# First x in four tiles, identity matmuls from the beginning, ctx's half of the gate sums ahead of x's, decode chunks and statistics placed anew

## The reference, cut to what matters

```
q = layernorm(x);  k = v = ctx                      # x, ctx: (8, 256, 512)
z = concat([q, k, v])                               # 1536 wide
ig, fg = z @ Wi + bi, z @ Wf + bf                   # the "gate sums": 2 x 16 columns
F = cumsum(log_sigmoid(fg));  log_D = tril(F_s - F_t) + ig_t
D = exp(log_D - max_t log_D);  C = (q @ k.T / sqrt(32)) * D     # per head
h = C / (max(|sum C|, exp(-max)) + 1e-6) @ v;  h = normed per head * ln_scale
x = x + h
w_gu, w_down = fp4(gate_up_packed) * scales, fp4(down_packed) * scales
g, u = split(layernorm(x) @ w_gu.T);  y = (silu(g) * u) @ w_down.T
out = x + y / rms(y)
```

## Time and profile before

| | |
|---|---|
| three runs | 546.90, 548.03, 548.43 us; median 548.03 |
| the profiled execution | 549.5 us, of it the span of the trace 547.8 us |
| mean granted clock of TensorE | 0.984 |
| PE busy | 507.3 us (93%) |
| DVE busy | 391.2 us (71%) |
| first feed-forward matmul of the span | 108.72 us after its start |

### The profile page before, as it was taken

The page is one execution under the profiler, slowest core; times in us unless marked ns, Lnnn a source line. Parts: engine busy times, 40 slices in busy tenths (PEclk is TensorE's granted clock), DMA queues, the critical chain, the costliest instruction groups (busy, mean ns, idle before and its releaser), DMA issues.

```text
span 547.8 us, 8218 instructions
## 1 busy us (share of the span) xinstructions
PE 507.3 (93%) x2752; PEld 280.2 (51%) x2752; DVE 391.2 (71%) x691; ACT 295.1 (54%) x639; POOL 332.2 (61%) x371
## 2 busy tenths in 40 slices
PE   0989996899999899999999999999999989989996
PEld 0556773436666345466665445566664443323442
DVE  4877878978888988277778898477778763877301
ACT  0355854387776352677767234787764224865000
POOL 1054446188887763667776883667768653888501
PEclk9988997999999999999999999999999999999999
DMA  8854037073103200456006001571000000200000
GB/s 270 245 175 167 9 109 256 33 258 136 40 2 134 97 0 2 130 186 225 0 7 227 0 1 41 193 269 39 2 1 1 19 20 25 90 1 1 20 19 38
DMA packets 22234, 47.81 MB, mean 87 GB/s; under 512 B 1840, under 2 KB 8880, under 8 KB 21680
## 3 DMA queue, kind: packets, MB, share of 16 engines
q1 hardware_dynamic: 22192, 47.28, 25.1%
HBM read 37.31 MB, written 4.33 MB: 76 GB/s over the span
## 4 chain that ended last, share of the span: by engine, by line
PE 73%; DVE 12%; ACT 5%; issue 4%; POOL 4%; DMA 1%; DVEq 0%; POOLq 0%; ACTq 0%
PE pf L993 25%; PE pf L979 18%; PE po L917 9%; PE pq L883 7%; PE pq L842 2%; PE pq L895 2%; PE pq L979 2%; PE pf L1012 2%; PE pq L922 2%; DVE ffn L1258 2%; ACT dmat L664 2%; DVE ffn L1262 1%; POOL hT L540 1%; ACT ts L698 1%; DVE bst L1081 1%
## 5 line engine op out<-in xcount | busy, mean ns | idle before, releaser
L993 PE MATMUL pf<-w_down,hT 128*128 128x512 f32 x352 | 154.0, 595 | 1.7 <-DVE w_down L1326 1.7
L979 PE MATMUL pf<-yT,gu_val 128*128 128x512 f16 x552 | 133.5, 380 | 4.5 <-DVE ffn L1262 1.7
L535 POOL TENSOR_TENSOR ffn<-ffn,ts 128x512 f32<-128x512 f32 x88 | 118.3, 1345 | 28.7 <-DVE ffn L1262 18.7
L698 ACT ACTIVATE ts<-pf,gu_scale 128x512 f32<-128x512 f32 x138 | 87.3, 684 | 46.8 <-PE pf L979 45.6
L993 PEld LDWEIGHTS pf<-w_down,hT 128*128 128x128 f32 x352 | 65.8, 190 | 83.8 <-issue 77.3
L979 PEld LDWEIGHTS pf<-yT,gu_val 128*128 128x128 f16 x552 | 49.9, 98 | 67.8 <-DVE ffn L1262 8.3
L664 ACT ACTIVATE dmat<-negm,aT 128x128 f32<-128x128 f32 x248 | 77.7, 396 | 0.8 <-DMA negm<-negm_dram 0.8
L540 POOL TENSOR_TENSOR hT<-ffn,th 128x512 f32<-128x512 f32 x44 | 57.7, 1314 | 28.9 <-DVE th L1271 28.9
L1258 DVE SCALAR_TENSOR_TENSOR ffn<-pf,gu_scale,ts 128x512 f32<-128x512 f32 x69 | 51.6, 748 | 32.7 <-PE pf L979 18.7
L917 PEld LDWEIGHTS po<-v_sb,dmat 128*128 128x128 f32 x512 | 62.1, 192 | 4.8 <-issue 0.4
L494 POOL TENSOR_SCALAR_AFFINE_SELECT dmat<-dmat 128x512 f32<-128x512 f32 x64 | 44.2, 705 | 27.1 <-ACT dmat L664 27.1
(11 more groups left out here) (124 smaller groups left out, 650.9 us busy)
## 6 DMA issues: line engine op xcount, KB each, us to landing
negm<-negm_dram SPq DMA_DIRECT2D x31, 512.0 KB, 5.2
ffn<-in_x SPq DMA_DIRECT2D x4, 1024.0 KB, 6.7
xT<-in_ctx_T SPq DMA_DIRECT2D x16, 256.0 KB, 6.0
ctx_sb<-in_ctx SPq DMA_DIRECT2D x4, 1024.0 KB, 5.7
x_sb<-in_x SPq DMA_DIRECT2D x4, 1024.0 KB, 5.5
x_res<-x_sb SPq DMA_DIRECT2D x4, 1024.0 KB, 5.4
out<-x_res SPq DMA_DIRECT2D x16, 256.0 KB, 2.2
ts<-in_gate_up_bytes SPq DMA_DIRECT2D x4, 352.0 KB, 9.5
```

The source lines that it names most:

```text
L535: pool.tensor_tensor(acc, acc, ts[:, h % TDEEP, 1], ALU.add).then_inc(tsum_ready, 1)
L698: act.activation(ts[:, h % TDEEP, g], bank(q, h, g), ACT.Copy, scale=gu_scale[:, g * GU + o:g * GU + o + 1]).then_inc(t_ready, 1)
L979: last = pe.matmul(bank(q, h, g), gu_val[:, h // 2 + h % 2 * FT, g], yT[:, part, g], start=(part == 0), stop=(part == 1))
L993: last = pe.matmul(pf[:, tt], hT[:, j, tt * P:(tt + 1) * P], w_down[:, j], start=(j == 0), stop=(j == FT - 1))
```

## The change

1. x of pair 0 is loaded by four transfers of one tile each, every one with its own semaphore (`load_first`), and each tile's statistics wait for its own tile.
2. ctxT comes in another layout (made on the host side of the program, as before) so that each pair is one transfer of 8 KB a partition. This holds for all pairs.
3. PE begins with 28 identity matmuls, does ctx's half of the gate sums, then the transposes of x, then x's half, and then 28 identity matmuls in place of 24.
4. `gate_weights` goes ahead of `norm1` on DVE. Two decode chunks (in place of four) stand before the gate rows, three more between `read_a(0)` and the first unit, and the loop's chunks start with chunk 5 in place of 4, so that they end one unit earlier.
5. The statistics of pair 1's x move from before the first unit to h = 9, 11, 13 and 15 of the loop; `shift1` moves from h = 15 to 17.
6. `head_sums` is split in two; in the first iteration the half of batch entry 0 stands at h = 17.
7. SP loads the scales and does `spread_negm(0)` before the words of the down projection, `ln_row` and pair 1's x.

```diff
-UP_FIRST = 4
-UP_EARLY = 4
+UP_FIRST = 2
+UP_EARLY = 5
 DOWN_CHUNKS = 4
 WORDS_AT = {1 + 2 * i: UP_EARLY + i for i in range(UP_CHUNKS - UP_EARLY + DOWN_CHUNKS)}
+STATS_AT = {9 + 2 * i: i for i in range(TT)}
...
-                for k in range(KT):
-                    sp.dma_start(xT[:, KT + k].rearrange("q (b s) -> q b s", b=2), ctxT_pairs[p][:, k]
-                                 ).then_inc(s_ctxT, 16)
+                sp.dma_start(xT[:, KT:2 * KT].rearrange("q k s -> q (k s)"), ctxT[p]).then_inc(s_ctxT, 16)
+
+            def load_first():
+
+                for tt in range(TT):
+                    sp.dma_start(xg[:, tt], x_pairs[0][:, tt]).then_inc(s_first[tt], 16)
...
-            load_xg(0, None)
+            load_first()
             sp.dma_start(w_gate[:], w_gates).then_inc(s_const, 16)
             sp.dma_start(bias_col[:], b_gates).then_inc(s_const, 16)
             load_gu(0)
             load_ctxT(0)
             load_ctx(0)
             load_gu(1)
-            load_xg(1, None)
             sp.dma_start(sc_raw[:], gu_scales).then_inc(s_scales, 16)
+            spread_negm(0)
             for half in range(2):
                 sp.dma_start(dn_words[half * HALF:(half + 1) * HALF].rearrange("p o w -> p (o w)"), dn_bytes
                              ).then_inc(s_down, 16)
             sp.dma_start(ln_row[:], ln_scale.partition_broadcast(P)).then_inc(s_ln, 16)
-            spread_negm(0)
+            load_xg(1, None)
             iteration(0, None, 1)
...
+            def first_sums(ks):
+
+                if ks[0] == KT:
+                    pe.wait_ge(wg_ready, 1)
+                    pe.wait_ge(s_ctxT, 16)
+                for k in ks:
+                    if k < KT:
+                        pe.wait_ge(xT_read, k + 1)
+                    last = gate_step(k, k == KT, k == KT - 1)
+                if ks[-1] == KT - 1:
+                    last.then_inc(g_done, 1)
...
             pe.wait_ge(const_ready, 2)
+            keep_busy(28, po[:])
+            first_sums(range(KT, 2 * KT))
             turn_x(0)
-            gate_sums(0)
-            keep_busy(24, po[:])
+            first_sums(range(KT))
+            keep_busy(28, po[:])
             spread_first(0)
...
-            def head_sums(p):
-                po_steps.start(p)
-                dve.wait_ge(osq_ready, 2 * p + 2)
-                po_steps.inc(dve.tensor_reduce(hn[:, 0], osq, AX.X, ALU.add))
+            def head_sums(p, b):
+                if b == 0:
+                    po_steps.start(p)
+                dve.wait_ge(osq_ready, 2 * p + 1 + b)
+                g = slice(b * 2 * NH, (b + 1) * 2 * NH)
+                po_steps.inc(dve.tensor_reduce(hn[:, 0, g], osq[:, g], AX.X, ALU.add))
...
-                    if q is None and h == 15:
+                    if q is None and h in STATS_AT:
+                        norm1_sums(n, (STATS_AT[h],))
+                    if q is None and h == 17:
                         shift1(n)
+                        head_sums(p, 0)
                 if q is None:
-                    head_sums(p)
+                    head_sums(p, 1)
                     head_scale(p)
...
             norm1_sums(0)
+            gate_weights()
             norm1(0)
-            gate_weights()
             for i in range(UP_FIRST):
                 decode_up(i)
             gate_rows(0)
...
             read_a(0)
-            norm1_sums(1)
+            for i in range(UP_FIRST, UP_EARLY):
+                decode_up(i)
             iteration(0, None, 1)
```

More of the change, by code:

```diff
@@ L112, in xattn_ffn @@
     ctx_pairs = ctx.rearrange("(p b) (c q) d -> p q (b c) d", b=2, q=P)
-    ctxT_pairs = ctxT.rearrange("(p b) (k q) s -> p q k b s", b=2, q=P)
     out_pairs = out.rearrange("(p b) (c q) d -> p q (b c) d", b=2, q=P)
@@ L232, in xattn_ffn @@
         s_x = sem("s_x")
+        s_first = [sem(f"s_first{i}") for i in range(TT)]
         s_xg = sem("s_xg")
@@ L330, in load_ctxT @@
                     sp.wait_ge(qk_done, UNITS * p)
-                for k in range(KT):
-                    sp.dma_start(xT[:, KT + k].rearrange("q (b s) -> q b s", b=2), ctxT_pairs[p][:, k]
-                                 ).then_inc(s_ctxT, 16)
+                sp.dma_start(xT[:, KT:2 * KT].rearrange("q k s -> q (k s)"), ctxT[p]).then_inc(s_ctxT, 16)
+            def load_first():
+                for tt in range(TT):
+                    sp.dma_start(xg[:, tt], x_pairs[0][:, tt]).then_inc(s_first[tt], 16)
             def load_xg(p, q):
-                if p > 0:
-                    sp.wait_ge(xT_done, KT * p)
+                sp.wait_ge(xT_done, KT * p)
                 sp.dma_start(xg, x_pairs[p]).then_inc(s_xg, 16)
@@ L831, in gate_sums, with gate_step @@
                 pe.wait_ge(xT_read, KT * (p + 1))
[L832 to L835, removed]
+                pe.wait_ge(s_ctxT, 16 * (p + 1))
+                if p > 1:
                     pe.wait_ge(acc_ready, 4 * FT * (p - 1))
                 for k in range(2 * KT):
[L839 to L843, removed]
-                last.then_inc(g_done, 1)
+                    last = gate_step(k, k == 0, k == 2 * KT - 1)
+                last.then_inc(g_done, 1)
+            def first_sums(ks):
[8 more added lines that the diff above has]
+                    last.then_inc(g_done, 1)
+            def gate_step(k, first, final):
+                for gate in range(2):
+                    for b in range(2):
+                        r = (2 * gate + b) * DH
+                        last = pe.matmul(pm[r:r + DH, 0:S], w_gate[:, k, gate * DH:(gate + 1) * DH],
+                                         xT[:, k, b * S:(b + 1) * S], start=first, stop=final)
+                return last
             def turn_back(p):
@@ L1087, in norm1_sums @@
                     g1.start(p)
-                    dve.wait_ge(s_xg, 16 * p + 16)
+                    if p > 0:
+                        dve.wait_ge(s_xg, 16 * p)
                 for tt in tiles:
+                    if p == 0:
+                        dve.wait_ge(s_first[tt], 16)
                     stats(g1, xg[:, tt], 0, tt)
@@ L1433 @@
     scales = _np.asarray(inputs["L0_ffn_gate_up_scales"]).reshape(KT, GU, HALF, 2)
+    ctx_T = _np.asarray(inputs["ctx_2048"]).reshape(PAIRS, 2, S, KT, P).transpose(0, 4, 3, 1, 2).reshape(PAIRS, P, KT * 2 * S)
     inputs = dict(
-        inputs, ctx_T=_np.asarray(inputs["ctx_2048"]).transpose(0, 2, 1), gate_weights=gates, gate_biases=biases,
+        inputs, ctx_T=ctx_T, gate_weights=gates, gate_biases=biases,
         gate_up_bytes=_np.ascontiguousarray(up.transpose(3, 0, 2, 1)).reshape(HALF, GU * KT * P).view(_np.int32),
```

## The result

The changed kernel is slower: median 554.05 us of four runs (553.49 to 554.62) against 548.23 (546.90 to 548.55), ratio 1.0111 with a 95% interval of 1.0089 to 1.0132. Ten runs of it over two sessions lie between 552.2 and 560.9.

A forecast was written before the change was run, and what follows sets the result against it. PE, busy 93% of the span, bounds the later iterations, so only the stretch before the first feed-forward matmul can move. Terms 2.0 - 0.3 - 0.7 - 1.4 + 3.1 = 2.7 us gained, median 548.03 to 545.3; range 541.6 to 547.8.

The forecast's parts named there:

- The start: Up to the end of pair 0's gate sums (G): G at 22.0 us, gain 2.0 (bounds 1.1 and 4.8).
- The 28 matmuls behind G: Identity matmuls after pair 0's gate sums: nearly hidden, 0.3 us lost (0 to 1.3).
- the high-clock rival: Clock stays high from the front matmuls: gate sums end at 19.2, time 542.2 us; chance 0.25.
- Three decodes before unit 0: DVE's decode chunks between the scans and unit 0: 0.7 us late (0 to 1.2).
- Statistics in the units: Pair 1's statistics in slots h = 9, 11, 13: 1.4 us lost (0.6 to 1.6), including a PE wait of 0.6.
- The last unit and head sums: From unit 7's products to the end of head sums: gain 3.1 us (2.3 to 3.3).
- The 1.15 for half of head sums: Half of head sums moves into DVE's wait for PE in the last unit: 1.15 of 2.29 us gained.
- SP's order: Order of SP's loads, with scales early: worth nothing.
- The slower one: Rival: the 28 identity matmuls behind the gate sums run slow and outlast the scans, 551.6 us; chance 0.08.

The follow-up runs named there:

- g2: e3 with the scales loaded ahead of pair 1's x, as in the changed kernel; 546.72 us, ratio 0.9970 to the kernel before.
- e2: The changed kernel with PE's list at the start as before the change (transposes, then all gate sums); 550.38 us, ratio 1.0037.
- g3: The changed kernel without the 28 identity matmuls in front, ctx's half still first; 553.52 us, ratio 1.0104.
- g4: g2 with PE's order of e2, three decode chunks ahead of the gate rows, one behind the scans, half of head sums at h = 17; 544.28 us, ratio 0.9938.
- f3: The changed kernel with 14 identity matmuls in place of 6 between unit 0's scores and its values; 550.76 us, ratio 1.0066.
- h1: g2 with pair 1's statistics at h = 9, 11, 13 and 15 and shift1 at h = 17; 552.78 us, ratio 1.0070.
- e3: The changed kernel with decodes, statistics and SP's order put back, head sums in two pieces behind the last step; 551.19 us, ratio 1.0066.
- the second profile: The changed kernel itself run and profiled once more, nothing changed; median 552.64 us, ratio 1.0089.
- e4: The kernel before with five decode chunks ahead of the gate rows, statistics in the units and head sums in halves; 551.78 us, ratio 1.0055.
- f2: The changed kernel with three decode chunks ahead of the gate rows and two behind the scans; 551.76 us, ratio 1.0008.

## Why the prediction was wrong

I forecast 545.3, in a range up to 547.8, and the time is 554.05. Point by point:

- *The start.* Right: G 22.2 where I had 22.0, nm 6.6 later, ctxT at 14.3 inside the bounds, ctx's half slow and x's half fast. g2 confirms the size (1.6). The 28 matmuls behind G lost nothing (0.3 forecast). The G of the high-clock rival (19.2) is real too, G at 18.5, but it comes from transposes in front and not from identity matmuls (e2, g3, g4).
- *Three decodes before unit 0: "I take 0.7 late (0 to 1.2)".* **This is the first step that failed.** Measured 3.5 (9.76 in place of 6.21, and within 0.01 of that in all five profiles with three chunks there). I took a decode's price from the units, 2.3, where GpSimd is busy for part of it. Beside the centring of v and the mask a chunk takes up to 3.9. The bound was drawn from rows of the wrong neighbourhood: at the place to which the chunks move, GpSimd is idle for only some 1.4 of the 9.8 us, and its own rows were there to be read.
- *What hangs behind.* The sum had no term for PE's clock after G. **That is the second failure, about as large.** The late products made PE pause 2.2 us, and the low stretch from 41.5 on cost 2.7 us more than before's own. With eight more identity matmuls in the pause (f3) this stretch is as long as before again in the profile, and the median 1.9 us lower.
- *Statistics in the units: "I take 1.4 lost (0.6 to 1.6)".* The direct price was 1.1, and the wait of 0.6 was where I said. But the same step costs 6.1 us in the median (h1 against g2). That the clock falls behind this wait is what h1's profile and six others show; that it makes the rest of the 6.1 us in all runs is argued, since one run of twelve was profiled in each. The term had the wait right and no price for the clock behind it.
- *The last unit and head sums: "Gain 3.1".* Up to the end of head sums 2.8 were gained, but only 2.1 at the first feed-forward. Counted from unit 7's products, it is 30.8 us to that matmul in place of 32.7, which is about the decode's 2.0 alone. **The 1.15 for half of head sums did not come:** `nb`, moved to h = 17, took 1.14 us beside GpSimd, so that both halves ran one after the other behind it, and `hn` L1224 behind them took 0.9 more. It is the failure of the three decodes again. PE's transposes of y also ran at the low clock (1.90 us for the first eight in place of 1.04), but that cost nothing: from the end of the `tok` that they wait for to the first feed-forward matmul it is 5.9 us in both kernels.
- *SP's order: "nothing".* Nothing waited for a load in the changed kernel, as I had it. But "nothing" was wrong as a price: with this start and the old order, nm is 2.2 us later and the median 4.5 higher (e3 against g2).
- *The rivals.* The slower one had the right kind of cause, the clock, at the wrong place: identity matmuls behind G took 6.2 us, fast throughout.

The terms that the two profiles show sum up to 5.1 us: -1.8, +3.5, +2.7, +1.1, -2.8, +0.7, -0.2, +1.9. The last is chance of that run. The forecast was a gain of 2.7 us, 7.8 away: 2.8 of that are the three decodes, 2.7 the clock behind them, 1.0 head sums, 1.9 chance; the other terms came out 0.6 better than forecast. That the second profile is as long (553.0) rests on other low stretches, 1.6 us of it in the units. What stays open: why the kernel before, which has four low stretches of its own up to the first feed-forward (the last, 108.0 to 111.4, in and behind a pause of PE of 2.1 us), is so steady (its mean granted clock lies between 0.979 and 0.990 in all but one of 88 runs in these sessions), while kernels with the statistics in the units range from 0.956 to 0.990. The waits in the units go with it, but they are not all of it: e3 has none and lies at 0.972 to 0.978, over 6.6 us. The runs don't show how short a wait is harmless.

## What to carry to other kernels

Price a moved instruction by rows from the place where it will stand, with the engines that are busy there, GpSimd above all for VectorE; a slot that looks idle on one engine can be the dearest of all. Where TensorE is on the path, price every new wait of it twice: its own length, and the low-clock stretch that may follow (3.4 to 13.7 us long in these profiles). Time such a change by many runs, since the one profile may be the lucky one, as e4's was. When a load is late, put work that doesn't need it in front of the wait, not matmuls without a purpose.

## What I had not expected of the hardware

- A wait of 0.62 us of PE in an otherwise full stretch was followed by 13.7 us at 1.2 GHz (h1, 62.8 to 76.5), with PE shown busy all the time; a pause of 0.45 us in f3 at 39.1 had no fall until 43.3, and e4 had the same wait of 0.63 us and no fall.
- The same kernel on the same chip ranged over 13.5 us (f2, 545.3 to 558.8), in step with its mean granted clock (0.990 to 0.957).
- Two-pass f32 matmuls with 33 columns lose much at the low level too: unit 0's values took 3.25 us, all but the first 0.4 at 1.2 GHz, in place of 1.87.
- A VectorE instruction on 128x4 numbers (`nb`) took 1.14 us beside GpSimd's multiplications in place of 0.15, and one on 128x64 (`hn` L1224) 1.10 in place of 0.23.
